# First layer of a two-layer attention and expert network: three engines' programs without loops, and the low parts of keys and queries on GpSimd

## What is computed

```python
x = x + xattn0(layernorm(x), ctx, ctx, mask_keys, Wq, bq, Wk, bk, Wv, bv, Wo, bo)  # 16 heads of 8
x = x + moe(layernorm(x), w_gate, w1, w2)            # 8 experts, the best 2 of each row
x = x + xattn1(layernorm(x), ctx, mask_queries, Wq, Wkv, Wout, bout)              # 16 heads of 64
x = x + ffn(layernorm(x), w1, b1, w2, b2)
```

```python
qm, km, vm = heads(q @ Wq.T + bq), heads(k @ Wk.T + bk), heads(v @ Wv.T + bv)
scores = where(mask, qm @ km.T / sqrt(8), -1e8)
out = (softmax(scores) @ vm) @ Wo.T + bo
```

## Time and profile before

| | |
|---|---|
| time, median of 3 runs | 938.54 us (936.50 to 940.93) |
| span of the profiled execution | 955.2 us |
| first stage in the profile | steps 4 to 27 (the loops) from about 58 to 305 us, single steps until about 362 us |
| busy over the span | PE 94%, DVE 70%, ACT 73%, POOL 47% |

### The profile page before, as it was taken

One profiled execution on the slowest core, in us unless ns is written; L12 is line 12 of the kernel. 1 busy time (PEld: TensorE's weight loads), 2 busy tenths in 40 slices (PEclk: granted clock), 3 DMA queues, 4 the chain that ended last, 5 costly groups with the idle time before them and its releaser, 6 DMA issues. The chain is left out here.

```text
span 955.2 us, 29952 instructions
## 1 busy us (share of the span) xinstructions
PE 896.2 (94%) x8399; PEld 785.4 (82%) x8399; DVE 673.3 (70%) x2146; ACT 694.9 (73%) x2694; POOL 446.4 (47%) x739
## 2 busy tenths in 40 slices
PE   5899999999999987999998799999999999999996
PEld 3677766777766777999997699999999999999995
DVE  5788887888888874222222788888787778777873
ACT  2888887888888962333335999998778877887882
POOL 4124433433433453111114777776666666666542
PEclk9999999999999998999999999999999999999998
DMA  5766656666666613222221122222112111211110
GB/s 156 226 212 198 214 186 201 201 204 200 208 214 208 196 41 92 72 71 67 67 92 53 34 62 62 63 68 62 61 45 66 60 59 45 66 60 57 41 51 10
DMA packets 113563, 103.93 MB, mean 109 GB/s; under 512 B 11761, under 2 KB 100627, under 8 KB 113494
## 3 DMA queue, kind: packets, MB, share of 16 engines
q1 hardware_dynamic: 106594, 88.81, 29.8%
q0 software_dynamic: 6112, 13.90, 4.7%
q10 hardware_dynamic: 788, 0.39, 0.1%
HBM read 56.53 MB, written 46.53 MB: 108 GB/s over the span
## 5 line engine op out<-in xcount | busy, mean ns | idle before, releaser
L664 ACT ACTIVATE PR<-PR,nmx 128x128 f32<-128x128 f32 x512 | 198.0, 390 | 8.1 <-DVE nmx L868 5.6
L664 ACT ACTIVATE PR<-bank,nmx 128x128 f32<-128x128 f32 x512 | 182.1, 384 | 6.6 <-issue 6.1
L334 POOL TENSOR_TENSOR PR<-PR,rden 128x512 f32<-128x512 f32 x128 | 133.7, 1044 | 92.2 <-DVE rden L873 85.8
L1149 PE MATMUL bank<-ident,PR 128*128 128x128 f32 x1024 | 156.7, 276 | 4.5 <-POOL PR L334 1.6
L1149 PEld LDWEIGHTS bank<-ident,PR 128*128 128x128 f32 x1024 | 118.8, 141 | 49.5 <-issue 40.8
L664 ACT ACTIVATION_READ_ACCUMULATOR PR<-bank,nmx 128x1 f32 x512 | 114.6, 224 | 0.0
L758 ACT ACTIVATE H<-bank 128x512 f32<-128x512 f32 x70 | 41.8, 597 | 90.4 <-PE bank L1355 90.4
L1383 PE MATMUL bank<-XCT,wqk 128*128 128x128 f32 x832 | 103.7, 278 | 0.7 <-ACT XCT L652 0.7
L1383 PEld LDWEIGHTS bank<-XCT,wqk 128*128 128x128 f32 x832 | 96.9, 192 | 3.5 <-ACT XCT L652 1.0
L664 ACT ACTIVATION_READ_ACCUMULATOR PR<-PR,nmx 128x1 f32 x512 | 96.8, 189 | 0.0
L868 DVE TENSOR_REDUCE nmx<-bank 128x4 f32<-128x512 f32 x128 | 86.6, 676 | 12.8 <-PE bank L1189 12.1
(11 more groups left out here) (196 smaller groups left out, 2092.2 us busy)
## 6 DMA issues: line engine op xcount, KB each, us to landing
second_layer_values<-wide SPq DMA_DIRECT2D x32, 512.0 KB, 3.0
wide<-second_layer_values SPq DMA_DIRECT2D x32, 512.0 KB
expert_outputs<-HF SPq DMA_DIRECT2D x32, 256.0 KB
expert_outputs<-HF SPq DMA_DIRECT2D x64, 128.0 KB, 1.9
KBD<-expert_outputs SPq DMA_DIRECT2D x128, 64.0 KB
QS<-expert_outputs SPq DMA_DIRECT2D x32, 256.0 KB
PR<-expert_inputs SPq DMA_DIRECT2D x36, 128.0 KB, 2.0
expert_outputs<-PR POOLq DMA_DIRECT2D x35, 128.0 KB, 2.0
```

Of the source, the lines that this page charges most:

```text
L334: nc.gpsimd.tensor_tensor(unit, unit, rden[:, p, G * g:G * g + G].unsqueeze(2).broadcast_to([P, G, P]), ALU.mult).then_inc(s["nm"], 1)
L664: last = nc.scalar.activation(PR[:, g, j * P:(j + 1) * P], scored, ACT.Exp, bias=nmx[:, p, h:h + 1], accum_out=den[:, p, h:h + 1])
L1149: last = nc.tensor.transpose(T_BANK[g % 2][:, j * P:(j + 1) * P], PR[:, g, j * P:(j + 1) * P], ident[:])
```

## The change

VectorE, ScalarE and GpSimd call a new `straight_steps`, which emits every step of the first stage one after the other with n a plain number. TensorE and SyncE keep their loops. `wait_apart` no longer waits for `const_ready` where all counts are plain numbers. The two subtractions that make low parts leave VectorE for GpSimd: that of the queries of n+1 is the first thing of GpSimd's step n, and that of the keys of n+2 comes behind both norms and ahead of L562 and the scatters. VectorE's L939 now waits for `kl` of the sequence before, and L948 for `ql` in place of `qh`.

```diff
--- before.py
+++ after.py
@@ -78,6 +78,16 @@
     if between:
         between(len(cuts) - 1)
     for n in range(2 * loop_end, last + 1):
+        step(n, n % 2)
+
+
+def straight_steps(step, first, last, ahead, behind, between=None, every=3):
+
+    loop_start, loop_end = (behind + 1) // 2, (NB - 1 - ahead) // 2
+    cuts = {2 * c: k for k, c in enumerate(list(range(loop_start, loop_end, every)) + [loop_end])}
+    for n in range(first, last + 1):
+        if between and n in cuts:
+            between(cuts[n])
         step(n, n % 2)
 
 
@@ -256,7 +266,8 @@
         def wait_apart(engine, *counts):
 
             counts = [(s, v if isinstance(v, int) else engine.to_reg(v)) for s, v in counts]
-            engine.wait_ge(const_ready, 1)
+            if not all(isinstance(v, int) for _, v in counts):
+                engine.wait_ge(const_ready, 1)
             for s, v in counts:
                 wait(engine, s, v)
 
@@ -571,6 +582,9 @@
 
             def step0(n, p):
                 q = 1 - p
+                if exists(n + 1):
+                    wait_apart(pool, (a["qh"], n + 2), (a["qw"], 32 * (n + 1)))
+                    nc.gpsimd.tensor_tensor(PARTS[:, 3, :].bitcast(FP32R), QC, PARTS[:, 2, :], ALU.subtract).then_inc(a["ql"], 1)
                 if exists(n - 1):
                     wait_apart(pool, (a["rd"], n), (a["rt"], n - 1))
                     nc.gpsimd.tensor_copy(RB[:].rearrange("p (t k d) -> p k t d", t=2, k=PAIRS),
@@ -580,6 +594,9 @@
                     norm_pool(pool, rt, n - 2, p)
                 if exists(n + 3):
                     norm_pool(pool, a, n + 3, q)
+                if exists(n + 2):
+                    wait_apart(pool, (a["kh"], n + 3), (a["kw"], 16 * (n + 2)))
+                    nc.gpsimd.tensor_tensor(PARTS[:, 1, :].bitcast(FP32R), KC, PARTS[:, 0, :], ALU.subtract).then_inc(a["kl"], 1)
                 if isinstance(n, int):
                     late_constants(n)
                 if not is_sequence(NB + 2, n):
@@ -588,7 +605,7 @@
                 else:
                     scatter_rows(n - 4, p)
                     keep_rows(n - 3, q)
-            over_steps(pool, step0, -3, NB + 3, 3, 4)
+            straight_steps(step0, -3, NB + 3, 3, 4)
 
 
             pool.wait_ge(rows_zeroed, 3)
@@ -716,7 +733,7 @@
                     wait(act, a["pv"], NU * (n))
                     nc.scalar.activation(diagonal(q), bank[4][:, 2 * P:3 * P].rearrange("p (k t d) -> p k t d", k=PAIRS, t=2),
                                          ACT.Copy).then_inc(a["vc"], 1)
-            over_steps(act, step0, -3, NB + 3, 3, 4)
+            straight_steps(step0, -3, NB + 3, 3, 4)
 
 
             def read_keys(m, half):
@@ -886,10 +903,6 @@
                 if exists(n - 4):
                     wait(dve, rt["hot"], n - 3)
                     nc.vector.tensor_tensor(chosen[:], hot1[:, 0, :], hot1[:, 1, :], ALU.add).then_inc(rt["chosen"], 1)
-                if exists(n + 1):
-                    dve.wait_ge(a["qh"], n + 2)
-                    wait(dve, a["qw"], 32 * (n + 1))
-                    nc.vector.tensor_tensor(PARTS[:, 3, :].bitcast(FP32R), QC, PARTS[:, 2, :], ALU.subtract).then_inc(a["ql"], 1)
                 if isinstance(n, int) and n == -1:
                     bias_rows()
                 if isinstance(n, int) and n in (0, 1, 2):
@@ -936,15 +949,14 @@
                     nc.vector.tensor_copy(scat_idx[:, p, :].unsqueeze(2), slot_f[:, :, bass.ds(n - 4, 1)]).then_inc(rt["placed"], 1)
                 if exists(n + 2):
                     dve.wait_ge(a["kq"], n + 3)
+                    wait(dve, a["kl"], n + 2)
                     nc.vector.scalar_tensor_tensor(KC, bank[4][:, 0:P], bqk[:, 1:2], mk_bc[:, bass.ds((n + 2) * P, P)],
                                                    ALU.add, ALU.mult).then_inc(a["kc"], 1)
                     dve.wait_ge(a["kc"], n + 3)
                     wait(dve, a["kw"], 16 * (n + 2))
                     nc.vector.tensor_copy(PARTS[:, 0, :].bitcast(FP32R), KC).then_inc(a["kh"], 1)
-                    dve.wait_ge(a["kh"], n + 3)
-                    nc.vector.tensor_tensor(PARTS[:, 1, :].bitcast(FP32R), KC, PARTS[:, 0, :], ALU.subtract).then_inc(a["kl"], 1)
                     dve.wait_ge(a["kq"], n + 3)
-                    wait(dve, a["qh"], n + 2)
+                    wait(dve, a["ql"], n + 2)
                     nc.vector.tensor_scalar(QC, bank[4][:, P:2 * P], float(DH0) ** -0.5, bqk[:, 0:1],
                                             ALU.mult, ALU.add).then_inc(a["qc"], 1)
                 if exists(n):
@@ -971,7 +983,7 @@
                     dve.wait_ge(a["rts"], n)
                     wait(dve, a["o"], n - 2)
                     nc.vector.tensor_tensor(OT0[:, q, :], O_BANK, RTS[:], ALU.mult).then_inc(a["oN"], 1)
-            over_steps(dve, step0, -3, NB + 3, 3, 4, late_inputs)
+            straight_steps(step0, -3, NB + 3, 3, 4, late_inputs)
 
 
             dve.wait_ge(rt["slots"], NB)
```

## The result

In the comparison that the prediction was for, the changed kernel takes 931.09 us (928.34 to 933.45, 9 runs) and the kernel before 938.54 (934.35 to 940.93, 9 runs): 0.9919 of it, with a 95% interval of 0.9900 to 0.9939. That is 7.5 us, inside the likeliest case's own range.

The account below looks back on a forecast made before the run. TensorE was taken to bind the first stage: 9.29 plus 0.1 for transfers is 9.39 against VectorE's 9.86, 0.47 over 24 steps, 11.3 us. 938.5 less 10.5 gave 928 us; likeliest range 921 to 933, overall 920 to 940.

Parts of the forecast that it names:

- likeliest case: First stage: hold-up mostly the profiler's, timed steps go from VectorE's 9.86 to TensorE's 9.29; 921 to 933 us, chance 0.45.
- 16.7 us of the span belong to the profiler: Whole kernel before: profiled span 955.2 us against 938.5 unprofiled, the 16.7 us difference put down to the profiler.
- VectorE's 9.86 as the starting point: First-stage loops before: VectorE's steps without their waits, 9.54 and 10.18, average 9.86 us, taken as the timed step.
- TensorE's 9.29 in loops against 8.97 straight: First stage: TensorE's own need per step, 9.29 us in its loops and 8.97 in straight steps.
- The loops: 0.75 on VectorE, 0.33 on the scatter chain: First-stage steps: writing loops out saves VectorE 0.75 us a step and the chain through the scatters 0.33, judged from step 28.
- the rival (10.01 a step, 936): First stage: the scatter chain binds timed runs too, step 10.01 us against 10.15, saving 2 to 3 us, 936; chance 0.35.
- L892 leaves VectorE, 0.20 on both paths; L945, 0.33 on VectorE: Subtractions leaving VectorE: L892, before L310, saves 0.20 us on VectorE and scatter chain; L945, behind L310, 0.33 on VectorE only.
- Subtraction of keys on GpSimd, 0.46: GpSimd between norms and scatters: adds 0.46 us to the scatter chain, bounds 0 and 0.85, nothing on VectorE's or TensorE's paths.
- The slower rival: GpSimd's subtraction of keys: at 0.85 us the scatter chain's step is 10.40 against 10.15, giving 945 us; chance 0.13.
- Which nobody else waits for before the experts: GpSimd behind the subtraction of keys: copy L562 and both scatters, claimed to keep no other engine waiting before the experts.
- Subtraction of queries, cost nothing: GpSimd behind the second scatter: costs nothing, store L469 no later; over half a microsecond late would delay the transfer to QS.
- Transfers, 0.1 a step: Transfers to QS: shorter steps uncover them now and then, adding 0.1 us a step to TensorE's 9.29.

Follow-up runs that it names:

- loops only: Changed kernel with both subtractions back on VectorE, so only the loops are written out: 937.2 us beside 956.9 for the kernel before, 0.9814, chip 7.
- moves only: Changed kernel with loops kept on VectorE, ScalarE and GpSimd, so only the two subtractions move: 955.0 us beside 956.9 for the kernel before, 0.9978, chip 7.
- experiment 7: Changed kernel with GpSimd's subtraction of keys moved behind the copy L573: 950.0 us beside 957.05 for the kernel before, 0.9931, chip 7.
- experiment 1: Kernel before, unedited, profiled a second time: 958.2 us beside 956.9 for the same kernel, ratio 1.0005, chip 7.
- experiment 3: The same run as moves only: changed kernel with loops kept on VectorE, ScalarE and GpSimd; 955.0 us beside 956.9 for the kernel before, 0.9978.

## Why the prediction came out right, and where it was wrong

**"16.7 us of the span belong to the profiler": wrong, and only luck kept the number right.** In every run of this study the span lies 1.6 to 3.1 us under the same execution's own time. The kernel before has two times, 957 to 958 us on chips 7 and 9 and 939 on chip 3 and in the first comparison, whose chip isn't recorded. The earlier trace rows were taken where it takes the long one. The text had the right two cases side by side and chose with the wrong reason: "the timed runs" and "the profile" came from executions with the words in time and with the words late, most likely on different chips. Had the comparison run on chip 7, the changed kernel would have taken 944, outside the 920 to 940 of the forecast, beside a before of 957. I had noticed that the span was longer than the times, which a span can't be, and explained it by the tool in place of doubting that both were of one state.

**The likeliest case, TensorE the bound with words in time: right in kind.** The changed kernel's step is TensorE's to within 0.1 or so, no word is late, and its time of 931 lies in the 921 to 933 given. The range was not well founded at its upper end: "with 9.54 for the average it is 931" doesn't follow from the text's own terms, since 9.54 less 9.39 is 0.15 a step, 3.6 us, which gives 935. Three terms were off.
- *VectorE's 9.86 as the starting point* was too high. The kernel before without scatters, the nearest stand-in for it in that state, has odd steps of 9.19 and even ones of 9.42 to 9.82, about 9.4 on average (no trace shows the kernel itself at 938). Part of what I had counted as VectorE's own work isn't there in that kernel: 0.2 us of issue behind the loop's end, and 0.25 at L960, which takes 0.41 in the loops of the trace before and 0.16 here. A scatter beside it isn't enough to bring that about: in step 28 L960 ran beside one and took 0.15. I did not find out what does.
- *TensorE's 9.29 in loops against 8.97 straight* was too far apart. The 6.43 that I took from the earlier trace rows ended with a wait for VectorE's L948. With that wait gone the loops cost it 0.06 on average (8.98 and 9.09 against 8.97), and writing them out gained 0.7 us of 927.6, which is nothing that can be measured. The 8.97 itself was exact.
- *The sum* was 0.47 a step, 11.3 us. Without the scatters it is about 0.34 a step and 9.0 us in the times; with them 7.5. The sign that VectorE would wait about 0.8 us more in a step did not come: it stands idle for 0.6 to 0.7 of a step of 9.18, where it was 1.1 of 9.84.

**The loops: 0.75 on VectorE, 0.33 on the scatter chain.** On the chain it is twice as much. Loops only brings the average over all 24 steps from 10.3 to 9.6, 16 of its 20 us. Step 28 was the wrong measure of a straight step: its VectorE part, less its 0.61 wait, was 4.39, and in loops only it is 4.20, with L892 still on VectorE; GpSimd started 0.17 behind L310 and starts 0.09 behind it in the written-out kernels, where `wait_apart` also no longer waits for `const_ready`. That term is why the rival (10.01 a step, 936) is too small: measured 9.83, and 12.7 us where the words are late.

**L892 leaves VectorE, 0.20 on both paths; L945, 0.33 on VectorE: only partly seen.** In loops, L892's leaving is worth what was forecast: moves only needs 4.24 and 4.67 up to the end of L321, where the kernel before needs 4.40 and 4.89. In straight steps it is no gain on the chain: loops only, which keeps it, needs 4.20 and the changed kernel 4.19. In both the first of VectorE's score maxima (L885) starts 1.46 after the step does (211.66 and 210.20; 208.43 and 206.97), 0.02 after the count of TensorE's scores goes up (1.44 into the step in both), so it is the scores that set it, and the freed 0.20 is spent waiting for them. VectorE has no difference of even and odd steps left, as forecast.

**Subtraction of keys on GpSimd, 0.46: right.** The upper bound of 0.85 was loosely added, since 0.46 and twice 0.16 are 0.78. The term itself is 0.46 by the record and 0.41 by the chain (5.02 less 4.61). In the late state it costs what it adds: 944.4 against 937.2 for loops only, on one chip. The slower rival, which needed 0.60, falls with it. By the ratio of 2 of the Trainium skill (GPSIMD Engine Reference, section 4.1) it would have been 0.58; the row ahead was nearer.

**"Which nobody else waits for before the experts": wrong.** VectorE's L328 writes the block that L573 copies, so it waits for it, 0.29 in most steps. The subtraction ahead of L573 is the cause, since the wait goes when it stands behind (experiment 7). In the state of the first comparison it took slack that VectorE had; whether it costs time there was not tried.

**Subtraction of queries, cost nothing: right for the transfers, with two costs on VectorE that I had not seen.** It ends 0.63 into a step (216.26 + 0.47 against 216.10), where VectorE's L892 ended 0.57 into one (step 19 before), so the store can leave at about the same place. But L905, which starts just after it (207.10 against 207.06), takes 0.46 in place of 0.15, until the end of L587. From step 6 to 28 it does so where L587 starts 25 to 46 ns ahead of it, and takes 0.15 where L587 starts 14 to 24 ns ahead (in one step L587 is 140 ns ahead, and L905 takes 0.36). This is the 0.1 us a step of the result's two kinds: behind a long L905, VectorE is 0.1 later at its first score maximum (L885 starts 1.54 into the step, though the count of the scores is up at 1.42), and TensorE's next scores are 0.1 later too (2.59 against 2.46). So "cost nothing" was wrong by about 0.1 us in over half of the steps. The Trainium skill (SBUF — State Buffer, section SBUF: two separate sides) says that VectorE, where its instruction has two inputs in SBUF, and GpSimd share a pair of ports which the one that comes first locks for its whole instruction; L905's 0.46 agrees with it. Its 0.15 in the steps where L587 comes first by 14 to 24 ns does not, unless the records are off by that little.

The other cost is L313, 0.68 in place of 0.34 in the changed kernel, in which it ends as L587 starts. What doubles it was not settled: beside a scatter in loops only it takes 0.34, and in experiment 7, where L587's like comes right behind the scatter as well, 0.34 in all but two steps.

**Transfers, 0.1 a step: right in kind.** TensorE waited for `QS` twice before, 1.27 us at 152.27 and 0.66 at 306.88, and twice after, 1.83 at 143.72 and 1.12 at 273.21. That is 1 us more in all, where the sum put 2.4. The first wait also varies from one execution to the next (1.58 in experiment 1).

Three things stay open. Some 4 to 6 us of the difference on chip 7 lie behind the first stage (from the last L973 to the end 609 and 610 us before, 605 changed), and were not followed; the 2 us of experiment 3 are of this kind, as its first stage takes as long as before. Of the state where the kernel before takes 939, no trace exists of it with its scatters. And neither loops only nor moves only was run in that state, so how the 7.5 us of the first comparison divide between the two parts isn't shown.

## What to carry to other kernels

A span that is longer than the times it is compared with is a sign that the two were taken in different states; look for the state, and work the sum out in both, before putting the difference down to the tool. An instruction's duration read in one state can hold time that belongs to that state: measure a step where nothing is late. And when work is moved to an idle engine, list who waits for each instruction behind it, the buffer it copies from included.

## What the hardware showed that I had not expected

- On chips 7 and 9, TensorE's counts go up late for most matmuls that run beside GpSimd's indirect scatters, by up to 2.4 us, in a burst some 0.4 to 0.65 us after the second scatter's end. TensorE itself goes on, as far as its records show. On these chips the kernel before takes 957 to 958 us and not 939. In the first comparison, with the same scatters beside the same matmuls, the delay was 0.02. What sets the chips apart is not known.
- The late words follow the scatters: at another place of the step they hit other matmuls' counts (up to 1.9 us late) and leave L1208's alone.
- Beside a subtraction on GpSimd that starts 25 to 46 ns earlier, a VectorE addition of 128 x 8 takes 0.46 to 0.48 us, and 0.15 where it starts 14 to 24 ns earlier (trace of the changed kernel, steps 6 to 28).
